# Cross-attention: both halves of the dense product together behind the fourth score unit, in place of one half on each side of it

## The reference, cut to what matters

```python
ci = rms_norm(hidden_states, ln_post_cross_w)
cq = heads(ci @ cq_w, NH, CHD)                  # 16 heads of 16
ckv = encoder_outputs @ ckv_w                   # 375 x 256 @ 256 x 512
ck, cv = jnp.split(ckv, 2, axis=-1)
ck, cv = (heads(ck, NH, CHD), heads(cv, NH, CHD))
cctx = sdpa(cq, ck, cv, causal=False)           # softmax(cq ck^T) cv
cctx = cctx.transpose(0, 2, 1, 3).reshape(b, l, CC)
hidden_states = hidden_states + cctx @ cdense_w # 112 x 256 @ 256 x 512: "dense"
```

## Time and profile before

| what | value |
|---|---|
| three timed runs | 2353.12, 2364.46, 2363.64 us; median 2363.64 |
| profiled execution, its own time | 2356.54 us |
| its span, first to last instruction | 2354.7 us |
| mean granted TensorE clock | 0.982 of full |
| busy: TensorE matmuls / weight loads | 2201.5 / 1835.8 us |
| busy: VectorE / ScalarE / GpSimd | 1339.2 / 1071.3 / 879.2 us |
| chain that ended last | TensorE 78%, VectorE 9%, ScalarE 7%, DMA 3% |
| cross-attention stage | about 1062 to 1640 us of the span |

### The profile page before, as it was taken

One profiled execution on the slowest core, in us unless ns is written; L12 is line 12 of the kernel. 1 busy time (PEld: TensorE's weight loads), 2 busy tenths in 40 slices (PEclk: granted clock), 3 DMA queues, 4 the chain that ended last, 5 costly groups with the idle time before them and its releaser, 6 DMA issues.

```text
span 2354.7 us, 46949 instructions
## 1 busy us (share of the span) xinstructions
PE 2201.5 (93%) x19542; PEld 1835.8 (78%) x19542; DVE 1339.2 (57%) x1919; ACT 1071.3 (45%) x1842; POOL 879.2 (37%) x738
## 2 busy tenths in 40 slices
PE   6899998999979999997999999998899999999998
PEld 5789986887756667886777777776888888888887
DVE  4655545878769994545666666663534444435332
ACT  4334434343157774433555555554543334434332
POOL 2201016677534333531121111110655455455553
PEclk8999999999989999997999999999999999999999
DMA  6434334565364436632111111111644343443331
GB/s 198 138 118 143 116 97 172 202 234 204 131 213 133 138 120 249 243 138 79 39 49 43 39 50 41 39 35 53 220 129 159 117 131 122 141 132 117 107 112 45
DMA packets 107058, 293.58 MB, mean 125 GB/s; under 512 B 14424, under 2 KB 18360, under 8 KB 100216
## 3 DMA queue, kind: packets, MB, share of 16 engines
q1 hardware_dynamic: 86624, 229.63, 30.1%
q0 software_dynamic: 18720, 60.29, 7.0%
q10 hardware_dynamic: 1504, 0.68, 0.1%
HBM read 221.36 MB, written 69.18 MB: 123 GB/s over the span
## 4 chain that ended last, share of the span: by engine, by line
PE 78%; DVE 9%; ACT 7%; DMA 3%; issue 2%; POOL 1%; SPq 0%; POOLq 0%; DVEq 0%; ACTq 0%
PE ps L109 19%; PE ps L111 18%; PE ps L110 18%; PE ps L1607 4%; PE ps L1626 3%; PE ps L1644 3%; DVE f_arena L979 3%; ACT f_arena L1529 2%; PE ps L1146 2%; ACT f_arena L1094 1%; DMA f_arena<-mem_n 1%; PE ps L620 1%; DVE f_arena L975 1%; DVE f_arena L971 1%; PE ps L1157 1%
## 5 line engine op out<-in xcount | busy, mean ns | idle before, releaser
L109 PE MATMUL ps<-r_arena 128*128 128x512 f32 (+6 forms) x2410 | 903.0, 375 | 38.1 <-DVE r_arena L177 20.5
L177 POOL TENSOR_TENSOR r_arena<-f_arena,r_arena 128x512 fp32r<-128x512 f32 (+1 forms) x438 | 587.4, 1364 | 870.1 <-ACT r_arena L1250 434.7
L111 PE MATMUL ps<-r_arena 128*128 128x512 f32 (+6 forms) x2410 | 882.0, 366 | 0.0
L110 PE MATMUL ps<-r_arena 128*128 128x512 f32 (+6 forms) x2410 | 881.9, 366 | 0.0
L109 PEld LDWEIGHTS ps<-r_arena 128*128 128x128 f32 (+2 forms) x2410 | 454.4, 189 | 130.5 <-issue 27.4
L111 PEld LDWEIGHTS ps<-r_arena 128*128 128x128 f32 (+2 forms) x2410 | 454.2, 188 | 65.9
L110 PEld LDWEIGHTS ps<-r_arena 128*128 128x128 f32 (+2 forms) x2410 | 455.0, 189 | 60.1
L199 ACT CAST r_arena<-f_arena 128x512 fp32r<-128x512 f32 x400 | 235.8, 621 | 174.2 <-PE ps L111 133.8
L1743 DVE TENSOR_REDUCE e_negmax<-ps 112x3 f32<-112x1125 f32 (+1 forms) x160 | 225.3, 1408 | 104.3 <-PE ps L1607 101.6
L1529 ACT ACTIVATE f_arena<-ps 125x1792 f32<-125x1792 f32 x96 | 159.8, 1665 | 98.4 <-PE ps L1629 98.0
L2029 DVE SCALAR_TENSOR_TENSOR f_arena<-f_arena,ps 128x512 f32<-128x512 f32 (+1 forms) x88 | 57.5, 653 | 233.9 <-ACT f_arena L1919 233.9
(11 more groups left out here) (201 smaller groups left out, 2734.2 us busy)
## 6 DMA issues: line engine op xcount, KB each, us to landing
f_arena<-weights SPq DMA_DIRECT2D x400, 256.0 KB, 3.0
f_arena<-rows SPq DMA_DIRECT2D x14, 1160.0 KB, 5.3
f_arena<-qk_rows SPq DMA_DIRECT2D x32, 448.0 KB, 3.9
f_arena<-mem_e SPq DMA_DIRECT2D x32, 376.0 KB, 3.2
f_arena<-mem_t SPq DMA_DIRECT2D x16, 750.0 KB, 9.5
f_arena<-mem_n SPq DMA_DIRECT2D x8, 1500.0 KB
h_rows<-f_arena SPq DMA_DIRECT2D x7, 1160.0 KB, 4.3
f_arena<-h_rows SPq DMA_DIRECT2D x7, 1160.0 KB, 5.4
```

What stands on the lines that cost most here:

```text
L109: first = pe.matmul(out, w_hi, x_hi, start=start, stop=False)
L110: pe.matmul(out, w_hi, x_lo, start=False, stop=False)
L111: return first, pe.matmul(out, w_lo, x_hi, start=False, stop=stop)
L177: return engine.tensor_tensor(out, source, high.bitcast(F32), ALU.subtract)
```

## The change

In each step s from 2 to 31, TensorE's stream has `dense(s - 2, 0)` behind `scores(s, 3)` and no longer ahead of it. `dense(s - 2, 1)` follows at once. No other engine's program changes, and neither does any wait.

```diff
--- before.py
+++ after.py
@@ -1703,10 +1703,9 @@
                 scores(s, 2)
                 if s:
                     scores_by_key(s - 1, 0)
+                scores(s, 3)
                 if s >= 2:
                     dense(s - 2, 0)
-                scores(s, 3)
-                if s >= 2:
                     dense(s - 2, 1)
                 if s:
                     scores_by_key(s - 1, 1)
```

## The result

The changed kernel takes 2365.84 us (median of 19 runs, 2362.4 to 2369.8), the kernel before 2358.88 us (19 runs, 2353.1 to 2365.1): the ratio is 1.0031, with a 95% interval from 1.0023 to 1.0040. It is 7 us slower, within 0.5%. The profiled execution took 2369.15 us, its span is 2367.3 us.

A forecast was written before the change was run, and what follows sets the result against it. TensorE, busy 93% of the span, was taken to bound the kernel, key unit 1 delaying each step. A new 0.66 us wait, net 0.35 us over 30 steps, adds 10.5 to 2359.4: 2370 us, range 2358 to 2380.

The forecast's parts named there:

- What bounds it: Cross-attention stage: TensorE's path through key unit 1 binds; the 0.38 us gap before score unit 3 is no wait for a maximum.
- Score unit 3 starts 0.06 us after the maximum: TensorE after the move: score unit 3 starts 0.06 us after unit 2's maximum ends, a new wait of 0.66 us.
- Joining the halves: TensorE before key unit 1: both dense halves together take 1.58 us instead of 1.77 apart, saving 0.19 us a step.
- The step: Steps 2 to 31: key unit 1 comes 0.35 us later, a step lasts 17.85 us; over 30 steps 10.5 us.
- Nothing given back: VectorE and ScalarE: score unit 3's earlier maximum (0.34 us) buys nothing, and the dense copy stays out of the way.
- The time: Whole kernel: 2359.4 us, the mean of four executions, plus 10.5 gives 2370 us, +0.45%.
- The score unit ready at once: Rival: score unit 3 is ready when key unit 0 ends; -0.31 us a step, -9.3 us, 2350 us; chance 4%.
- Absorbed on ScalarE: Rival: copy and chunk work on ScalarE set the exponent's start, so the delay costs nothing; 2359 us; chance 5%.
- The clock falls: Rival: pauses in a step halve TensorE's clock for 4 us stretches; 60 us if in all steps, 2430 us; chance 4%.
- The wait real already: Rival: score unit 3 already waits, starting at least 0.40 us after the maximum; +0.69 us a step, 2380 us; chance 4%.

The follow-up runs named there:

- Experiment 2: The kernel before with the maximum of unit 2 taken over 176 of 375 keys: 2356.86 us against 2356.79 for the kernel before, ratio 1.0000.
- experiment 4: The changed kernel with one additional matmul between key unit 0 and score unit 3: 2369.10 and 2369.07 us, ratios 1.0047 and 1.0048 to the kernel before.
- experiment 5: The kernel before with both dense halves together ahead of score unit 3: 2363.73 us against 2356.79 for the kernel before, ratio 1.0026.
- experiment 8: The changed kernel, unchanged, run twice again beside the kernel before: 2365.29 us against 2360.39, then 2367.35 against 2355.92.
- experiment 1: The changed kernel with the maximum of unit 2 taken over 176 of 375 keys: 2350.13 us against 2356.79 for the kernel before, ratio 0.9966.
- experiment 6: Both dense halves ahead of score unit 3, and the maximum of unit 3 over 176 of 375 keys: 2348.90 us against 2360.39 before, ratio 0.9954.

## Why the prediction was right

**What bounds it.** Right: dense half 0 covered the maximum, and nothing waited for it although the profile said so. Experiment 2 shows it by the ratio of 1.0000, experiment 4 by the hole that opened.

**Score unit 3 starts 0.06 us after the maximum.** Right: 1318.69 to 1318.75, and the wait is 0.66 us as forecast.

**Joining the halves.** Right: from the start of the first half to key unit 1 it was 1321.02 - 1319.44 = 1.58 us, the very sum taken from the tail of the stage.

**The step.** Key unit 1 was forecast 2.94 us behind key unit 0's loads and stands at 2.93 in the step shown; the step was forecast at 17.85 us and lasts 17.86 to 17.89. So the 0.35 us a step was a little short of 0.38, and 10.5 us for the stage short of 11.4. The remainder is 0.03 us a step, and it lies in the choice of one step for all. The step that I took has 2.59 us from key unit 0's loads to key unit 1; the mean over 28 steps is 2.57 before and 2.94 after, 0.37 us apart. The maximum ends 0.60 us behind key unit 0's loads in that step and 0.61 in the mean.

**Nothing given back.** Right for the key units and exponents, all later by the same amount. In the eight steps with a ring chunk score unit 4 moved by only 0.09 us (3.72 to 3.81 us behind key unit 0's loads), since the copy had held it up before; it stands in the shadow of the exponent, so that gave nothing back either. But I judged the slack of the chain through VectorE by one waiting pair (maximum 3 and score unit 4) and never added it up to score unit 0 of the next sequence. In this direction it did no harm, since score unit 3 came earlier. In experiment 5 the same omission made the expectation wrong.

**The time.** The forecast of 2370 us is 4 us over the median of 2365.84; the profiled execution took 2369.15. The base was right (2359.4 against 2358.88). The difference of the medians, 7.0 us, is less than the 10.5 forecast and even less than the 8.7 us that I gave as the lower end of the cost; the time stays in the range by the room that it left for scatter. The steps cost 11.4 us, inside 8.7 to 16.2. What lies between 7.0 and 11.4 is put down to the granted clock of the runs, which experiment 8 shows for two further sets of runs and not for this one.

**The rivals.** The score unit ready at once: refuted in the true kernel, and its mechanism shown by experiment 1. Its forecast of -9.3 us was also somewhat too good: -0.24 us a step, and none in the eight steps with a chunk. Absorbed on ScalarE: refuted, the exponent kept its 0.50 us of waiting for key unit 1. The clock falls: it didn't come, 1.00 over all steps in three profiles of the changed kernel, with pauses of 0.66 and 1.58 us in each. Of all the traces one shows a fall between 1104 and 1600, that of experiment 6 (0.57 in 1232 to 1236, after 4 us with TensorE busy 2.87), at a cost of 1.6 us; its cause isn't shown. By the Trainium skill (TensorE: Matmul & The Clock Gate, "A second HAM failure mode: psum-queue depth-cycling") short pauses between groups can make the clock swing; no run here shows that for a pause of this length. The wait real already: refuted by experiment 2.

## What to carry to other kernels

A piece of work between two dependent units is cover for the result that the second one waits for; before moving it, subtract the end of the producer from the end of what would be left in front. Add up every chain that passes the moved place to the same later point, through each engine: here TensorE with ScalarE and TensorE with VectorE lay within half a microsecond, so a move either way uncovered one of them. A releaser's name on a gap proves nothing: compare the gap with the same kind of gap where no such wait exists, or find a step in which the new order already runs.

## What the runs showed of the hardware

Weight loads of one unit can run among those of the unit before: in experiment 5 the first load of key unit 1 stands at 1301.10, beside the last three of score unit 3, and key unit 1 began 0.3 us earlier than a sum over whole units gave. Its last load came less than 0.1 us earlier than by that sum (3.15 us behind key unit 0's loads, for 2.26 + 0.95): while the loads of the two units are mixed, key unit 1's take 1.19 us in place of 0.95. The Trainium skill (TensorE: Matmul & The Clock Gate, "The mechanism") says that a load for rows that don't conflict is pulled ahead of matmuls in flight; the trace agrees here. By the code (`r = slice(32 * (h % 4), ...)`) score unit 3, heads 9 to 11, uses the rows from 32 on, and the load that came forward is for rows 0 to 31. The traces showed nothing of it between score units and the dense halves. Matmuls changed places as well:

```profile
1301.10 0.36 PE L1626 MATMUL ps<-r_arena 32*125 32x224 f32 x1
1301.10 0.50 PE L1607 MATMUL ps<-r_arena 32*112 32x376 f32 x5
```

Key unit 1 stands behind score unit 3 in the program, but its first matmul starts at 1301.10 and the last three of score unit 3 at 1301.27, and so it is, by at least 0.16 us, in all steps from 2 to 30. The order of matmuls that the prediction assumed didn't hold between these two units.

The mean granted clock of one and the same kernel ran from 0.978 to 0.984 among 24 runs on one chip, and the times with it from about 2363 to about 2354 us. A difference of a few us between medians needs the clocks beside it.
